# A batch's preparation spread over two steps of a software-pipelined attention and FFN kernel

## The chip, the cores and the metric

One core of one Trainium2 chip. The metric is the device time of one execution in microseconds (us), as the median of several runs. In what follows PE is TensorE, DVE is VectorE, ACT is ScalarE, POOL is GpSimd and SP is SyncE.

## The reference

The input x has 8 batches of 1024 tokens with 128 channels. Cut to what matters:

```python
def proj(W, b): return heads(x + x @ W.T + b)          # 16 heads of 8 channels
q, k1, k2, v1, v2 = proj(Wq, bq), proj(Wk1, bk1), ...
S1 = k1^T v1 / n; S2 = k2^T v2 / n                      # per head, over all 1024 tokens
y1 = q @ S1 * mean(v2); y3 = q @ S2 * mean(v1)
y2 = (S1 * S2).sum(rows); y4 = q @ (S1 * S2)
a = layernorm(y1 * g1 + y2 * g2 + y3 * g3 + y4 * g4) * ln_g + ln_b
x = layernorm(x + a @ Wo.T + bo)                        # "x1"
h = relu(x @ w1[0] + b1[0]); e = h @ w2[0] + b2[0]      # only expert 0 has weight
out = layernorm(layernorm(x + e) * gamma + beta)        # "y2", "y3", "res"
```

S1 and S2 are sums over all tokens of a batch. They are computed from the batch's Gram matrix x^T x (128x128) and its column sums. The attention of a batch then collapses to one 128x128 matrix P, applied to each token.

## The kernel before, in words

**Groups and steps.** A group is 512 tokens (four tiles of 128), so there are two groups to a batch and 16 in all. The program is a loop over steps n = -2 to 15, unrolled, written once for each engine. Each engine has its own instruction stream, runs it strictly in the written order, and the streams are tied by semaphores alone. In step n the engines work on several groups: `product(n+1)` (x of group n+1 times PQ, 16 matmuls into `z_ps`), `up(n, 0..3)` (the FFN's first layer of group n, three matmuls each), `turn_x(n+2)` (four transposes into `turn_ps`), the down projection of group n (16 fp32 products that the profile counts as 32), and `turn_x1(n+1)`. In the odd steps 1, 3 and 5 a Gram matrix (of batches 5 to 7) follows the down projection, in two halves around `turn_x1`.

**Preparation.** Batch b is prepared in the even step n = 2b - 2 (b = 2 to 7), in this chain:

- `split_G(b)` on POOL writes `G_hi` and `G_lo`, the Gram matrix in two parts, at the end of the even step before;
- `gram_av(b)` on PE (three matmuls into `prep_ps`, in the middle of `product`) waits for both parts;
- `e_and_v(b)` on DVE writes `E_sb`, in the middle of the normalization to `y2n`;
- `ak_e(b)` on PE (after `up(n, 0)`) waits for `E_sb`; `s_out(b)` on DVE writes `S_sb`;
- `prepare(b)` on POOL: gv, then S12, T, S12g, M_half and `M_sb`, all small elementwise instructions, at the head of POOL's step;
- `attention_matrix(b)` on PE (after half of the down projection) waits for `M_sb`; `PT_copy` on ACT; `centered(b)` on PE waits for that copy; `PQ_upper` on ACT and `PQ_rest` on DVE give PQ, which `product` of the next step needs.

**POOL's order in a step.** `prepare` (even steps), `result_bias(n-2)` (L532 `mr4`, L535 `nb4`; in odd steps it comes after y3), y2g (L567), y3 (L571), `xu` (L584), x1b2 (L595), x1beta (L597), and in even steps `split_G` (L549, L551). `result_bias(n-2)` waits for DVE's `rstd4` (L852).

**DVE's order around `rstd4`.** `xT_rest(n+2)` (L834, waits for ACT's `xT_hi`, which waits for `turn_x`), `rstd2` (L939), `rstd4` (L852), the normalization to `x1` (L821), `PQ_rest`, `add_y2(n)` (L865, waits for the down projection), statistics, x1T_lo (L963), then the next step's `rstd3`, `y2n`, y3 statistics, `s_out`, `rstd1` and so on.

**ACT's order.** std3, four squares, std1, four ReLUs (L708, `hT`), `xT_hi` (L699), std2 and std4, `PT_copy` (L677), `PQ_upper` (L683), the result (L690), `x1T_hi` (L757).

All matmuls stand on L1045 in the profile, since the helper `mm` issues them; the tile's name tells them apart.

Of the kernel before, what the change touches and what calls it, by code (L numbers as in the profile page):

```python
# [35 lines left out]
SEQ_TILES = SEQ // TILE  # L36
# [10 lines left out]
def build(nc, x, Wq, bq, Wk1, bk1, Wk2, bk2, Wv1, bv1, Wv2, bv2, g1, g2, g3, g4, ln_g, ln_b, Wo, bo,  # L47
# [11 lines left out]
    with ctx:  # L59
# [45 lines left out]
        warm = sb("warm", [128, 1])  # L105
        minus = sb("minus", [128, TILES])
# [85 lines left out]
        const_set = sem("const_set")  # L192
        consts = sem("consts")
# [64 lines left out]

        end_y2 = sem("end_y2")
# [144 lines left out]
        class Step:  # L404
            def __init__(self, n):

                self.n, self.s = n, n % 2

                def has(k):
                    return 0 <= n + k < GROUPS  # L410

                self.cur, self.prev, self.prev2 = has(0), has(-1), has(-2)
                self.last = n == GROUPS - 1
                self.nxt, self.nxt2 = has(1), has(2)

                self.prep = n == -1 or (n != 0 and n % 2 == 0 and has(2))
                self.ready = 1 if n == 0 else self.prepared() if self.prep and n != -1 else None
                self.gram = EARLY + n // 2 if n in (1, 3, 5) else None
                self.v_set = {0: 0, 7: 1}.get(n)
                self.v_rest = {0: 0, 7: 1}.get(n)  # L420

            def prepared(self):

                return self.n + 2 if self.n < 0 else self.seq(2)

# [16 lines left out]
        def _(sp):  # L442
# [25 lines left out]
            def store(b):  # L468
                for g in range(1 if b == BATCHES - 1 else SEQ_GROUPS):
                    if (b, g) in ((0, 0), (2, 1)):  # L470
                        place_v(b // 2)
                    wait(sp, res_out, b * SEQ_GROUPS + (g + 1))
                    sp.dma_start(out_v[b, :, g * TILES:(g + 1) * TILES, :], res[g][:, :, :]).then_inc(res_free[g], 16)
# [13 lines left out]
        def _(pool):  # L487
# [65 lines left out]
            def body(st):  # L553
# [10 lines left out]
                if st.prev:  # L564

                    wait(pool, y2n_out, n)
                    pool.tensor_tensor(y2g[:, :, :], y2n[:, :, :], rows(gamma_rows[:, :]), ALU.mult).then_inc(y2g_out, 1)  # L567
                    wait(pool, y2g_out, n)
                    wait(pool, x1beta_out, n)
                    wait(pool, res_out, n - 2)  # L570
                    pool.tensor_tensor(y3[(s - 1) % 2][:, :, :], y2g[:, :, :], x1beta[(s - 1) % 2][:, :, :], ALU.add).then_inc(y3_out, 1)  # L571
                if st.prev2 and not st.prep and not st.last:
                    result_bias(n - 2)
                if st.nxt2:

                    m = n + 2
                    b, g = st.seq(2), s
                    pool.wait_ge(x_loaded[b], 16)
                    if n == -1:
                        pool.wait_ge(x0_second, 16)  # L580
                    if st.n == -2:
                        pool.wait_ge(u_ready, 1)
                    wait(pool, y1_out, m - 1)
                    pool.tensor_tensor(xu[s % 2][:, :, :], X[:, b, g * TILES:(g + 1) * TILES, 0:C],  # L584
                                       rows(u_rows[:, :]), ALU.add).then_inc(xu_out, 1)
                if st.n == -1:
                    prepare(pool, 1)
# [11 lines left out]
                if st.cur and n % 2 == 0 and n // 2 + 2 < BATCHES:  # L599
                    split_G(n // 2 + 2)  # L600

# [3 lines left out]
            pool.wait_ge(y3_out, GROUPS - 1)  # L605
# [8 lines left out]
        def _(act):  # L614
# [94 lines left out]

            def body(st):  # L710
# [12 lines left out]
                if st.cur:  # L723
                    if st.n == 0:
                        act.wait_ge(ffn_rows, FFN_ROWS)
                    relu(st, 0)
                    relu(st, 1)
                    if st.last:
                        root3(n)
                    relu(st, 2)  # L730
                    relu(st, 3)
# [13 lines left out]
                if st.prep:  # L745
                    PT_copy(st.prepared())
# [25 lines left out]

            half_std(st3, std3, 0, end_st3, end_std3)
            act.wait_ge(end_nb, 1)
            act.wait_ge(y2g_out, GROUPS - 1)
# [3 lines left out]
            root4(GROUPS - 2)  # L779
# [8 lines left out]
        def _(dve):  # L788

            dve.wait_ge(consts, 2)  # L790
# [52 lines left out]
            def y3_stats(m, buf):  # L843
                wait(dve, y3_out, m + 1)
                wait(dve, mr4_out, m)
                stats(lambda i: pairs(y3[buf], i), st4, st4_out)
# [20 lines left out]

            def e_and_v(b):
# [16 lines left out]
            def body(st):  # L885
                n, s = st.n, st.s
                if st.prev:

                    wait(dve, std3_out, n)
                    dve.reciprocal(rstd3[:, :], std3[:, :]).then_inc(r3_out, 1)  # L890
                    wait(dve, r3_out, n)
                    wait(dve, y2g_out, n - 1)
                    normalize(y2n, y2_tile, st3, rstd3, y2n_out, (lambda: e_and_v(st.prepared())) if st.prep else None)
# [13 lines left out]
                if st.prep and st.n >= 0:  # L907
                    s_out(dve, st.prepared())
# [42 lines left out]
                if st.ready is not None and st.n >= 0:  # L951
                    PQ_rest(st.ready)
                if st.cur and st.nxt2:
                    add_y2(n, s)
# [70 lines left out]

            half_y2(0)
            half_r3(0)
            dve.scalar_tensor_tensor(out=nb_end[:, half[0]], in0=st3[:, 0, 1:6:3], scalar=-1.0,
                                     in1=rstd3[:, half[0]], op0=ALU.mult, op1=ALU.mult).then_inc(end_nb, 1)
            y3_stats(GROUPS - 2, 1 - own)  # L1030
            half_y2(1)
            y2d_second()
            result_factors(GROUPS - 2)
            result_bias_here(GROUPS - 2)
# [8 lines left out]
        def _(pe):  # L1043
# [3 lines left out]
            def keep_warm(times):  # L1047

                for _ in range(times):
                    mm(up_ps[1][:, 0:128], ident[:, :], ident[:, :])  # L1050
# [35 lines left out]
            def gram(b, tiles):  # L1086
# [8 lines left out]
                if b >= EARLY:  # L1095
                    pe.wait_ge(PQfix_out, b - EARLY + 2)
                for t in tiles:
# [19 lines left out]
            def gram_av(b):  # L1117

                if b >= 2:

                    wait(pe, G_out, min(BATCHES, b + 4))
                    if b == 5:
                        pe.wait_ge(rows_out, 2)
# [13 lines left out]
            def v_rows(v):  # L1137
# [3 lines left out]
                if v == 1:  # L1141
                    pe.wait_ge(PQfix_out, 5)
                mm(rows_bank(v)[0:VSET, 0:256], G_sb[:, b:b + VSET, C], A_kv[:, 1:3, :].rearrange("p j c -> p (j c)")).then_inc(rows_done, 1)

            def attention_matrix(b):

                wait(pe, M_out, (b + 1) * 2)
                pe.wait_ge(AqT_ready, 2)
                mm(prep_ps[:, 0:XW], M_sb[:, :], AqT[:, :], start=True, stop=False)
# [57 lines left out]
            def body(st):  # L1207
                n, s = st.n, st.s
                if st.n == -2:
                    pe.wait_ge(consts, 1)  # L1210
                    keep_warm(6)
# [21 lines left out]
                if st.n == -1:  # L1233
                    gram(2, range(2, 4))
                    product(0, 0)
                    turn_x(1)
                    gram(2, range(4, SEQ_TILES))
# [7 lines left out]
                if st.nxt:  # L1245
                    product(n + 1, st.seq(1), (lambda: gram_av(st.prepared())) if st.prep else None)
                if st.cur:
                    up(n, 0)
                if st.prep:
                    ak_e(st.prepared())  # L1250
                if st.v_set is not None:
                    v_rows(st.v_set)
                if st.cur:
                    up(n, 1)
                    up(n, 2)
                    up(n, 3)
                if st.nxt2:
                    turn_x(n + 2)
                if st.cur:
# [5 lines left out]
                    for t in range(TILES):  # L1265
# [3 lines left out]
                        if t == 2 and st.prep:  # L1269
                            attention_matrix(st.prepared())  # L1270
                        for k in range(FCH):
                            if t == 2 and k == 2 and st.prep:
                                centered(st.prepared())
                            if t == 0:
                                wait(pe, relu_out, n * FCH + (k + 1))
                            last = mm(to, hT[:, k, t * TILE:(t + 1) * TILE], w2_sb[:, k, :],
# [37 lines left out]
```

## Time and profile before

| | |
|---|---|
| median of 3 runs | 203.22 us (203.04 to 203.26) |
| the profiled execution | 202.93 us, of which the span from first to last instruction is 201.2 us |
| busy share of the span | PE 95%, DVE 78%, POOL 70%, ACT 64% |
| mean granted TensorE clock | 0.984 of full speed |

"Busy" is the time in which an engine has at least one instruction under way. The ends of matmuls are modelled and neighbours overlap, so a PE that waits a tenth of a microsecond still looks busy. Of one step that has room for nothing else, only the sum of its pieces tells whether PE waited.

### The profile page before, as it was taken

Reading aid. Unit: us, or ns where it says so; the run is one execution under the profiler, and the core shown is the slowest. Engines: PE = TensorE matmul, PEld = TensorE weight load, DVE = VectorE, ACT = ScalarE, POOL = GpSimd, SP = SyncE. Lnnn points to the kernel's source line nnn. Section 1 sums busy time; section 2 is a strip of 40 time slices with the busy share of each in tenths; the row PEclk is TensorE's granted clock in tenths of the full one; section 3 lists DMA queues with packets and bytes.
Section 4 is the critical chain, followed back from the end, with each engine's and each line's share of the span. In section 5 each row is a group of like instructions: output and inputs, shape, how many; then the busy total and the mean of one; then the engine's idle time right before and its main releaser. Section 6 shows DMA issues by size and latency. Waiting matters only on the chain.

```text
span 201.2 us, 4296 instructions
## 1 busy us (share of the span) xinstructions
PE 190.6 (95%) x1369; PEld 174.4 (87%) x1369; DVE 156.9 (78%) x470; ACT 129.1 (64%) x386; POOL 141.6 (70%) x191
## 2 busy tenths in 40 slices
PE   6999999999999999999999999999999999999930
PEld 6898979999898989999997989898989899988820
DVE  0286717988879796988879896989698969897683
ACT  0433456553859565975768685867597759786852
POOL 8627490675599838984698859985998598876450
PEclk9999999999999999999999999999999999999985
DMA  5999502000001100101010300110010101010012
GB/s 169 199 285 286 134 0 82 3 2 3 0 3 49 55 2 0 57 0 52 3 52 28 104 3 0 54 53 4 0 52 5 52 3 52 2 52 30 25 54 104
DMA packets 12641, 10.64 MB, mean 53 GB/s; under 512 B 730, under 2 KB 10475, under 8 KB 12619
## 3 DMA queue, kind: packets, MB, share of 16 engines
q1 hardware_dynamic: 11960, 9.32, 15.0%
q0 software_dynamic: 352, 0.92, 2.2%
q8 instruction: 11, 0.18, 0.4%
q10 hardware_dynamic: 306, 0.13, 0.2%
q14 instruction: 12, 0.09, 0.2%
HBM read 6.17 MB, written 4.20 MB: 52 GB/s over the span
## 4 chain that ended last, share of the span: by engine, by line
PE 86%; DVE 6%; issue 3%; POOL 2%; ACT 1%; DVEq 0%; POOLq 0%
PE down_ps L1045 25%; PE up_ps L1045 25%; PE z_ps L1045 14%; PE prep_ps L1045 13%; PE turn_ps L1204 3%; PE turn_ps L1175 3%; DVE st L814 1%; DVE down_ps L865 1%; POOL y2g L567 1%; POOL y L571 1%; DVE z_ps L925 1%; ACT res L690 1%; DVE y2n L821 1%; PE z_ps L1055 0%; DVE res L1022 0%
## 5 line engine op out<-in xcount | busy, mean ns | idle before, releaser
L1045 PE MATMUL down_ps<-w_sb,hT 128*128 128x128 f32 x480 | 58.9, 276 | 0.1
L1045 PEld LDWEIGHTS down_ps<-w_sb,hT 128*128 128x128 f32 x480 | 56.4, 192 | 0.7 <-ACT hT L708 0.3
L708 ACT ACTIVATE hT<-up_ps,cols 128x512 f32<-128x512 f32 x64 | 42.2, 682 | 5.2 <-PE up_ps L1045 5.0
L690 ACT ACTIVATE res<-y,nb,rstd 128x128 f32<-128x128 f32 x60 | 24.8, 483 | 6.6 <-POOL nb L535 5.9
L595 POOL TENSOR_TENSOR x1b<-x,b_rows 128x512 f32<-128x512 f32 x16 | 20.6, 1286 | 10.4 <-DVE x L821 10.4
L1045 PE MATMUL up_ps<-x1T_hi,w_hi 128*128 128x512 f32 x64 | 26.1, 408 | 0.0
L1045 PE MATMUL up_ps<-x1T_lo,w_hi 128*128 128x512 f32 x64 | 25.4, 398 | 0.0
L1045 PE MATMUL up_ps<-x1T_hi,w_lo 128*128 128x512 f32 x64 | 25.3, 395 | 0.0
L567 POOL TENSOR_TENSOR y2g<-y2n,gamma_rows 128x512 f32<-128x512 f32 x15 | 19.2, 1282 | 4.8 <-DVE y2n L821 4.8
L821 DVE TENSOR_SCALAR x<-z_ps,st,rstd 128x128 f32<-128x128 f32 x64 | 21.9, 404 | 0.1
L657 ACT ACTIVATE z_sq<-z_ps 128x128 f32<-128x128 f32 x64 | 16.8, 270 | 7.7 <-PE z_ps L1045 7.7
L821 DVE TENSOR_SCALAR y2n<-down_ps,st,rstd 128x128 f32<-128x128 f32 x60 | 21.0, 403 | 0.5
L584 POOL TENSOR_TENSOR xu<-X,u_rows 128x512 f32<-128x512 f32 x16 | 19.0, 1189 | 2.4 <-DVE u_rows L810 2.4
L597 POOL TENSOR_TENSOR x1beta<-x,beta_rows 128x512 f32<-128x512 f32 x16 | 20.6, 1289 | 0.0
L571 POOL TENSOR_TENSOR y<-y2g,x1beta 128x512 f32<-128x512 f32 x15 | 19.1, 1272 | 1.2
L1045 PE MATMUL z_ps<-PQ_hi,xT_hi 128*128 128x256 f32 x64 | 19.3, 302 | 0.0
L925 DVE SCALAR_TENSOR_TENSOR z_ps<-z_ps,rstd,xu 128x128 f32<-128x128 f32 x64 | 18.1, 352 | 0.6
L1045 PE MATMUL z_ps<-PQ_hi,spread 128*128 128x256 f32 x64 | 18.0, 281 | 0.1
L1045 PE MATMUL z_ps<-PQ_hi,xT_lo 128*128 128x256 f32 x64 | 18.1, 282 | 0.0
L1045 PE MATMUL z_ps<-PQ_lo,xT_hi 128*128 128x256 f32 x64 | 18.0, 282 | 0.0
L649 ACT ACTIVATE std<-st,eps_col 128x4 f32<-128x4 f32 x46 | 12.4, 295 | 7.0 <-DVE st L814 7.0
L757 ACT ACTIVATE x1T_hi<-turn_ps 128x512 fp32r<-128x512 f32 x16 | 9.4, 589 | 11.2 <-PE turn_ps L1175 10.9
(170 smaller groups left out, 417.0 us busy)
## 6 DMA issues: line engine op xcount, KB each, us to landing
out<-res SPq DMA_DIRECT2D x15, 256.0 KB, 2.0
X<-in_L_attn_x SPq DMA_DIRECT2D x7, 512.0 KB, 8.7
V_all<-V_dram SPq DMA_DIRECT2D x6, 128.0 KB, 3.0
X<-in_L_attn_x SPq DMA_DIRECT2D x2, 256.0 KB, 3.5
w_sb<-in_L_ffn_w POOLq DMA_DIRECT2D x2, 256.0 KB, 7.8
out<-res SPq DMA_DIRECT2D x2, 128.0 KB, 2.2
w_raw<-in_L_attn_Wv ACTq DMA_DIRECT2D x2, 64.0 KB, 2.3
w_raw<-in_L_attn_Wk SPq DMA_DIRECT2D x2, 64.0 KB, 3.2
```

Of the source, the lines that this page charges most:

```text
L567: pool.tensor_tensor(y2g[:, :, :], y2n[:, :, :], rows(gamma_rows[:, :]), ALU.mult).then_inc(y2g_out, 1)
L571: pool.tensor_tensor(y3[(s - 1) % 2][:, :, :], y2g[:, :, :], x1beta[(s - 1) % 2][:, :, :], ALU.add).then_inc(y3_out, 1)
L584: pool.tensor_tensor(xu[s % 2][:, :, :], X[:, b, g * TILES:(g + 1) * TILES, 0:C], rows(u_rows[:, :]), ALU.add).then_inc(xu_out, 1)
L595: pool.tensor_tensor(x1b2[(s + 1) % 2][:, :, :], x1[:, :, :], rows(b2_rows[:, :]), ALU.add).then_inc(x1b2_out, 1)
L597: pool.tensor_tensor(x1beta[(s + 1) % 2][:, :, :], x1[:, :, :], rows(beta_rows[:, :]), ALU.add).then_inc(x1beta_out, 1)
L649: act.activation(dst[:, :], src, ACT.Sqrt, bias=eps_col[:, :], scale=scale).then_inc(done, 1)
L657: act.activation(z_sq[:, t, :], z_ps[t // 2][:, t % 2 * 256:t % 2 * 256 + C], ACT.Square, accum_out=z_sum[:, t:t + 1]).then_inc(sq_out, 1)
L690: last = act.activation(res[buf][:, t, :], y3[buf][:, t, :], ACT.Identity, scale=rstd4[:, t:t + 1], bias=nb4[:, t:t + 1])
L708: act.activation(hT[:, k, :], up_ps[k % len(up_ps)][:, :], ACT.Relu, bias=cols[:, 5 + k:6 + k]).then_inc(relu_out, 1)
L821: last = dve.tensor_scalar(dst[:, t, :], of_tile(t), st[:, t // 2, 3 * (t % 2) + 1:3 * (t % 2) + 2], rstd[:, t:t + 1], ALU.subtract, ALU.mult)
L925: last = dve.scalar_tensor_tensor(out=y1_tile(t), in0=y1_tile(t), scalar=rstd1[:, t:t + 1], in1=xu[(s + 1) % 2][:, t, :], op0=ALU.mult, op ...
L1045: return pe.matmul(o, lhsT, rhs, start=start, stop=stop)
```

## The change

The three parts of the preparation that make E and S move to the odd step before (n = 2b - 3, `st.pre` and `early()`): `gram_av` in its `product`, `ak_e` after its `up(n, 3)`, `e_and_v` in its `y2n`, `s_out` before its `add_y2`. `prepare` stays at the head of POOL's even step. `attention_matrix` moves up to stand between `up(n, 3)` and `turn_x`, `PT_copy` between the ReLUs and `xT_hi`, and `centered` before the second quarter of the down projection. `split_G` moves ahead of x1b2 and x1beta in POOL's even step. The second set of V rows, and its trip through DRAM on SP's queue, move from step 7 to step 6. At the start, seven warming matmuls on a tile that DVE sets take the place of six on `ident`, and `product(0)` comes two Gram tiles later. At the end, DVE makes y3 of group 14 (`y2d_before`, `y3_before`) where POOL did, the last ReLU is cut into two halves, and DVE takes the statistics of that y3 before the half sums of group 15.

The diff, cut to its core:

```diff
         self.ready = 1 if n == 0 else self.prepared() if self.prep and n != -1 else None
+        self.pre = n % 2 == 1 and n > 0 and self.seq(3) < BATCHES
         self.gram = EARLY + n // 2 if n in (1, 3, 5) else None
-        self.v_set = {0: 0, 7: 1}.get(n)
-        self.v_rest = {0: 0, 7: 1}.get(n)
+        self.v_set = {0: 0, 6: 1}.get(n)
+        self.v_rest = {0: 0, 6: 1}.get(n)
...
         return self.n + 2 if self.n < 0 else self.seq(2)
+    def early(self):
+        return self.seq(3)
...
         for g in range(1 if b == BATCHES - 1 else SEQ_GROUPS):
-            if (b, g) in ((0, 0), (2, 1)):
+            if (b, g) in ((0, 0), (2, 0)):
                 place_v(b // 2)
...
             result_bias(n - 2)
-        if st.prev:
+        if st.prev and not st.last:
...
                                rows(u_rows[:, :]), ALU.add).then_inc(xu_out, 1)
+        if st.cur and n % 2 == 0 and n // 2 + 2 < BATCHES:
+            split_G(n // 2 + 2)
         if st.n == -1:
...
-        if st.cur and n % 2 == 0 and n // 2 + 2 < BATCHES:
-            split_G(n // 2 + 2)
     run_steps(body)
...
     pool.wait_ge(end_y2n, 1)
-    pool.wait_ge(y3_out, GROUPS - 1)
+    pool.wait_ge(y3_out, GROUPS - 2)
     pool.tensor_tensor(y2g[:, 0:2, :], y2n[:, 0:2, :], rows(gamma_rows[:, :], 2), ALU.mult).then_inc(end_y2g, 1)
...
         act.activation(hT[:, k, :], up_ps[k % len(up_ps)][:, :], ACT.Relu, bias=cols[:, 5 + k:6 + k]).then_inc(relu_out, 1)
+    def relu_half(st, k, h):
+        part = slice(h * GROUP // 2, (h + 1) * GROUP // 2)
+        wait(act, up_done, st.n * FCH + (k + 1))
+        act.activation(hT[:, k, part], up_ps[k % len(up_ps)][:, part], ACT.Relu,
+                       bias=cols[:, 5 + k:6 + k]).then_inc(relu_out, 1)
...
             relu(st, 2)
-            relu(st, 3)
+            if st.last:
+                for h in range(2):
+                    relu_half(st, 3, h)
+            else:
+                relu(st, 3)
+        if st.prep and st.n >= 0:
+            PT_copy(st.prepared())
         if st.nxt2 and st.n >= 0:
...
             root4(n - 2)
-        if st.prep:
+        if st.prep and st.n < 0:
             PT_copy(st.prepared())
...
+    root4(GROUPS - 2)
     half_std(st3, std3, 0, end_st3, end_std3)
     act.wait_ge(end_nb, 1)
-    act.wait_ge(y2g_out, GROUPS - 1)
+    act.wait_ge(y2g_out, GROUPS - 2)
     for t in range(2):
...
     last.then_inc(end_y2n, 1)
-    root4(GROUPS - 2)
     half_std(st3, std3, 1, end_st3, end_std3)
...
+    dve.memset(warm_in[:, :], 1.0).then_inc(warm_set, 1)
     dve.wait_ge(consts, 2)
...
     def y3_stats(m, buf):
-        wait(dve, y3_out, m + 1)
+        if m == GROUPS - 2:
+            dve.wait_ge(y3_last, 1)
+        else:
+            wait(dve, y3_out, m + 1)
         wait(dve, mr4_out, m)
...
                           x1b2[s % 2][:, :, :], ALU.add).then_inc(y2_out, 1)
+    def y2d_before(m):
+        wait(dve, sq_out, GROUPS * TILES)
+        wait(dve, std1_out, GROUPS)
+        wait(dve, st3_out, m + 1)
+        for t in range(TILES):
+            last = dve.scalar_tensor_tensor(out=y2d[:, t, :], in0=y2_tile(t),
+                                            scalar=st3[:, t // 2, 3 * (t % 2) + 1:3 * (t % 2) + 2],
+                                            in1=gamma_rows[:, :], op0=ALU.subtract, op1=ALU.mult)
+        last.then_inc(y2d_out, 1)
+    def y3_before(m, buf):
+        dve.wait_ge(y2d_out, 1)
+        wait(dve, x1beta_out, m + 1)
+        wait(dve, res_out, m - 1)
+        for t in range(TILES):
+            last = dve.scalar_tensor_tensor(out=y3[buf][:, t, :], in0=y2d[:, t, :],
+                                            scalar=rstd3[:, t:t + 1], in1=x1beta[buf][:, t, :],
+                                            op0=ALU.mult, op1=ALU.add)
+        last.then_inc(y3_last, 1)
...
         n, s = st.n, st.s
+        if st.last:
+            y2d_before(n - 1)
         if st.prev:
...
             wait(dve, r3_out, n)
+        if st.last:
+            y3_before(n - 1, (s - 1) % 2)
+        if st.prev and not st.last:
             wait(dve, y2g_out, n - 1)
-            normalize(y2n, y2_tile, st3, rstd3, y2n_out, (lambda: e_and_v(st.prepared())) if st.prep else None)
+            normalize(y2n, y2_tile, st3, rstd3, y2n_out, (lambda: e_and_v(st.early())) if st.pre else None)
         if st.prep and st.n == -2:
...
             split_w1()
-        if st.prep and st.n >= 0:
-            s_out(dve, st.prepared())
         if st.n == -2:
...
             PQ_rest(st.ready)
+        if st.pre:
+            s_out(dve, st.early())
         if st.cur and st.nxt2:
...
+    y3_stats(GROUPS - 2, 1 - own)
     half_y2(0)
+    result_factors(GROUPS - 2)
+    result_bias_here(GROUPS - 2)
     half_r3(0)
...
                              in1=rstd3[:, half[0]], op0=ALU.mult, op1=ALU.mult).then_inc(end_nb, 1)
-    y3_stats(GROUPS - 2, 1 - own)
     half_y2(1)
     y2d_second()
-    result_factors(GROUPS - 2)
-    result_bias_here(GROUPS - 2)
     y3_second()
...
         for _ in range(times):
-            mm(up_ps[1][:, 0:128], ident[:, :], ident[:, :])
+            mm(up_ps[1][:, 0:128], warm_in[:, :], warm_in[:, :])
...
             pe.wait_ge(PQfix_out, b - EARLY + 2)
+            pe.wait_ge(S_out, b - EARLY + 3)
         for t in tiles:
...
-            wait(pe, G_out, min(BATCHES, b + 4))
-            if b == 5:
-                pe.wait_ge(rows_out, 2)
+            wait(pe, G_out, min(BATCHES, b + 3))
             if b == 2:
...
         if v == 1:
-            pe.wait_ge(PQfix_out, 5)
+            pe.wait_ge(S_out, 5)
         mm(rows_bank(v)[0:VSET, 0:256], G_sb[:, b:b + VSET, C], A_kv[:, 1:3, :].rearrange("p j c -> p (j c)")).then_inc(rows_done, 1)
...
         pe.wait_ge(AqT_ready, 2)
+        if b >= 2:
+            wait(pe, G_out, min(BATCHES, b + 4))
+        if b == 4:
+            pe.wait_ge(rows_out, 2)
         mm(prep_ps[:, 0:XW], M_sb[:, :], AqT[:, :], start=True, stop=False)
...
         if st.n == -2:
+            pe.wait_ge(warm_set, 1)
+            keep_warm(7)
             pe.wait_ge(consts, 1)
-            keep_warm(6)
             pe.wait_ge(consts, 2)
...
         if st.n == -1:
-            gram(2, range(2, 4))
+            gram(2, range(2, 6))
             product(0, 0)
             turn_x(1)
-            gram(2, range(4, SEQ_TILES))
+            gram(2, range(6, SEQ_TILES))
             gram(3, range(SEQ_TILES))
...
         if st.nxt:
-            product(n + 1, st.seq(1), (lambda: gram_av(st.prepared())) if st.prep else None)
+            product(n + 1, st.seq(1), (lambda: gram_av(st.early())) if st.pre else None)
         if st.cur:
             up(n, 0)
-        if st.prep:
-            ak_e(st.prepared())
         if st.v_set is not None:
...
             up(n, 3)
+        if st.pre:
+            ak_e(st.early())
+        if st.prep:
+            attention_matrix(st.prepared())
         if st.nxt2:
...
                     turn_x1(n + 1, False)
-                if t == 2 and st.prep:
-                    attention_matrix(st.prepared())
                 for k in range(FCH):
-                    if t == 2 and k == 2 and st.prep:
+                    if t == 1 and k == 0 and st.prep:
                         centered(st.prepared())
...
                         wait(pe, relu_out, n * FCH + (k + 1))
+                    if st.last and t == 2 and k == 0:
+                        pe.wait_ge(relu_out, GROUPS * FCH + 1)
                     last = mm(to, hT[:, k, t * TILE:(t + 1) * TILE], w2_sb[:, k, :],
```

## Rows read from the trace of the kernel before

**Rows 1.** The page's chain by engine, and all of PE's waits (total, times, longest).

```profile
PE 86%; DVE 6%; issue 3%; POOL 2%; ACT 1%; DVEq 0%; POOLq 0%
...
PE up_ps L1045 <- POOL ident L492: 1.6, 1, 1.6
```

**Rows 2.** Chain that ended last, steps 9 and 10: start, us, what (from end to end).

```profile
125.20 1.89 PE z_ps L1045 x16
...
129.90 0.44 PE turn_ps L1204 x4
130.34 3.57 PE down_ps L1045 x32
...
134.35 0.94 PE z_ps L1045 x8
135.29 0.36 PE prep_ps L1045 x3
...
137.33 0.71 PE prep_ps L1045 x4
...
142.37 0.49 PE prep_ps L1045 x4
...
143.42 0.95 PE prep_ps L1045 x4
...
146.14 0.24 PE z_ps L1045 x2
```

**Rows 3.** The same chain, in step 1: half a Gram matrix.

```profile
45.48 0.90 PE prep_ps L1045 x8
```

**Rows 4.** Timeline of POOL, steps 9 and 10: start us, us, what, and idle before.

```profile
128.03 0.28 POOL L549 CAST G_hi<-G_sb 128x128 fp32r<-128x128 f32 x1
128.39 0.46 POOL L551 TENSOR_TENSOR G_lo<-G_sb,G_hi 128x128 fp32r<-128x128 f32 x1
...
132.13 0.20 POOL L532 TENSOR_TENSOR mr<-st,rstd 128x4 f32<-128x4 f32 x1 [0.68 <-DVE rstd L852]
...
136.21 0.74 POOL L376 TENSOR_TENSOR gv<-V_all,gmask 128x256 f32<-128x256 f32 x1
139.18 0.46 POOL L380 TENSOR_TENSOR S<-S_sb 128x128 f32<-128x128 f32 x1 [2.23 <-DVE S_sb L361]
...
141.75 0.46 POOL L396 TENSOR_TENSOR M_sb<-M_half,S12g 128x128 f32<-128x128 f32 x1
142.31 0.20 POOL L532 TENSOR_TENSOR mr<-st,rstd 128x4 f32<-128x4 f32 x1
...
145.32 1.20 POOL L584 TENSOR_TENSOR xu<-X,u_rows 128x512 f32<-128x512 f32 x1
```

**Rows 5.** Timeline of all engines in step 10, from `turn_x` to `rstd4`.

```profile
139.99 0.60 PE L1204 MATMUL turn_ps<-ident,X 128*128 128x128 f32 x4
...
140.77 0.59 ACT L699 ACTIVATE xT_hi<-turn_ps 128x512 fp32r<-128x512 f32 x1
...
142.09 0.15 DVE L852 RECIPROCAL rstd<-std 128x4 f32<-128x4 f32 x1
```

**Rows 6.** The same chain, at the start: the first half of Gram matrix 0.

```profile
4.51 1.73 PE prep_ps L1045 x8
```

**Rows 7.** PE's weight loads in step -1: the one for `turn_x1(0)`.

```profile
25.37 0.42 PEld L1175 LDWEIGHTS turn_ps<-ident,x 128*128 128x128 f32 x4 [0.37 <-DVE x L821]
```

**Rows 8.** Timeline of DVE, the last step and what follows it.

```profile
187.41 0.16 DVE L852 RECIPROCAL rstd<-std 128x4 f32<-128x4 f32 x1
...
190.94 0.43 DVE L982 TENSOR_TENSOR prep_ps<-prep_ps,x1b 128x256 f32<-128x256 f32 x1 [1.08 <-PE prep_ps L1045]
...
192.59 0.76 DVE L814 BATCH_NORM_STATS2 st<-y 128x6 f32<-128x256 f32 x2
...
194.26 0.61 DVE L996 SCALAR_TENSOR_TENSOR z_sq<-z_ps,st,gamma_rows 128x128 f32<-128x128 f32 x2
...
195.91 0.76 DVE L1014 BATCH_NORM_STATS2 st<-y 128x6 f32<-128x256 f32 x2
```

More of the change, by code:

```diff
@@ L105, in build @@
         warm = sb("warm", [128, 1])
+        warm_in = sb("warm_in", [128, 128])
         minus = sb("minus", [128, TILES])
@@ L192, in build @@
         const_set = sem("const_set")
+        warm_set = sem("warm_set")
         consts = sem("consts")
@@ L257, in build @@
         res_out = sem("res_out")
+        y2d_out = sem("y2d_out")
+        y3_last = sem("y3_last")
         end_y2 = sem("end_y2")
```

## The prediction

> **What bounds the kernel now.** I read the chain that ended last and the table of waits first. The chain is 86% PE, and PE's only listed wait is the one for `ident` at the start [rows 1]. From the first step to the last, the time is therefore the sum of what PE is given plus small waits hidden in its pieces. So I read the chain for two steps without a Gram matrix, 9 and 10 [rows 2]. An odd step takes 134.35 - 125.20 = 9.15 us: product, up, `turn_x`, down, `turn_x1`. Both steps take 146.14 - 125.20 = 20.94. Twice 9.15 is 18.30; the other 2.64 is the preparation: `gram_av` 0.36, `ak_e` 0.71, attention 0.49, `centered` 0.95 and some 0.13 of switching. The 0.71 for four passes is long: four transposes of the same width take 0.44. Some 0.2 to 0.3 is a wait for `E_sb`.
>
> Next I read POOL's timeline [rows 4], because POOL sits between the two halves of the preparation. It idles 2.23 before S12, until `S_sb` is there, then ends `M_sb` at 142.21 and goes straight on to `mr4` at 142.31. The question for the change is where this idle time goes. Last, the way from `turn_x` to `rstd4` over ACT and DVE [rows 5], because `mr4` waits for `rstd4` and all of POOL's step stands behind `mr4`.
>
> **The preparation on PE.** Apart from a warming matmul, nothing is added to PE's work; blocks move. `ak_e` behind `up(n, 3)` no longer waits (`E_sb` is two microseconds old) and no longer splits the up products. I take 0.40 for it, 0.40 for attention (up to 0.49 now, with a short wait), 0.95 and 0.36 for the others: 2.11 in place of 2.64, so 0.5 less in each of the three pairs without a Gram matrix (steps 7 to 12). In the three pairs with one, PE comes later to `ak_e` and mostly the split is saved: 0.15 each. Together **-1.9** (bounds -1.2 and -2.4).
>
> **First new wait: attention for `M_sb`.** In the new order the chain from `turn_x` of the odd step is:
>
> - `turn_x` to `mr4`: now 142.31 - 139.99 = 2.32 [rows 4, 5]. ACT starts `xT_hi` 0.78 after `turn_x` because the fourth ReLU runs first. With `ak_e` or attention ahead of `turn_x`, that ReLU is done up to 0.4 sooner in relation to it. So the bounds are 1.9 and 2.3; I take 2.15, since the transposes need most of that time themselves.
> - `mr4` to the head of `prepare` (nb4, xu, x1b2, x1beta): 136.21 - 132.13 = 4.08 [rows 4].
> - `prepare` without its wait: 0.74 for gv, and from S12 to the end of `M_sb` 142.21 - 139.18 = 3.03: 3.77. It is not moved, and its length does not change. What goes is the wait for S alone.
> - 0.07 to hand over, as from `rstd4` to `mr4` [rows 4, 5].
>
> Together 10.07. PE gets from `turn_x` to the new place of attention in one bare step, 9.15: down, `turn_x1`, product, up. So PE waits **0.92** in steps 8, 10 and 12. In steps 2, 4 and 6 the Gram matrix of the step before gives PE two times 0.90 more [rows 3], 10.95 in all, and nothing is left to wait for. Behind attention stand `turn_x`, down and everything else of PE; they all slip.
>
> **Second new wait: `gram_av` for `G_lo`.** `split_G` used to have a step in hand; now `gram_av` follows in the next product. From `turn_x` of the even step: 2.15 to `mr4`; `mr4` to the end of `xu` 146.52 - 142.31 = 4.21; `split_G` 128.85 - 128.03 = 0.82; hand-over 0.07: 7.25. POOL's 2.2 of idle time is not won: it moves from before S12 to before `mr4`. PE's way is 135.29 - 129.90 = 5.39 plus `centered` 0.95 = 6.34 [rows 2]. PE waits **0.91** in steps 3, 5, 7, 9 and 11 (batches 3 to 7; batch 2 is split in step 0, long before). Behind it stand half the product, up and `turn_x`, so the first chain starts later by as much and does not get shorter.
>
> Sum of the waits: 3 x 0.92 + 5 x 0.91 = **+7.3**. Over eight waits the bounds 1.9 and 2.3 give 5.3 to 8.5.
>
> **Cover of the rest.** DVE gives up 1.0 in even steps and has it in odd ones; `s_out` fits in its wait for the down projection, and PE reaches `turn_x` later there, so it still waits for `xT_hi`. If that cover failed, `rstd4` would slip by up to 0.4. `PT_copy` has `turn_x` and a quarter of down (0.44 + 0.9) before `centered`, against 0.9 needed. The V rows and SP's three loads come a step before `gram_av(5)` and two before their use; SP stores nothing earlier for it. The Gram matrices' new wait for `S_out` ends as down ends (0 to 0.2, three times; I take 0).
>
> **The ends.** At the start PE can begin about 0.5 sooner, but the seventh warming matmul fills most of it. The first Gram half runs at 1.73 for eight passes, against 0.90 later [rows 3, 6]; if PE comes to the fast pace sooner, up to 0.5 is won. The two Gram tiles ahead of `product(0)` fill PE's wait for PQ, but `turn_x1(0)` already waits 0.37 for DVE [rows 7] and would only wait longer: 0. I take **-0.3** (0 to -0.6). At the end DVE's way from its first half sum to the statistics of y3 is 195.91 - 190.94 = 4.97 [rows 8]. The y3 statistics (0.7) leave it, and `rstd4` with its bias fills the wait for std3. DVE needs eight instructions of 0.3 (0.61 for two) more beforehand. From 187.6 that is 2.4 + 0.2 + 0.7, which ends at about 190.9, just in time. **-0.8** (-0.3 to -1.0). PE's gain from the half ReLU, about 0.3, is hidden behind DVE.
>
> **Sum.** The profiled execution took 202.93; + 7.3 - 1.9 - 0.3 - 0.8 = 207.2, span 205.5. The median shown is 0.29 above it, so **207.4** for the median, with a range of its own of 205.0 to 209.2.
>
> **Rivals.**
>
> - *It does what it says* (faster). No wait comes in the place of the old ones, and the 3.0 of savings stay: 200.2. For it: PE is the bound, and POOL idles 2.2 per pair. It needs POOL's results 0.9 sooner than the rows give, for instance `turn_x` to `mr4` in 1.25 rather than 2.15. Against it: POOL's chain is one instruction after another. 14%.
> - *Only `gram_av` waits*, because `prepare` profits from something that I do not see: 203.2 + 4.55 - 3.0 = 204.8. 14%.
> - *Only attention waits*, because `split_G` is sooner: 203.2 + 2.8 - 3.0 = 203.0, between a little faster and the same. 5%.
> - *The waits bring the clock down.* The mean granted clock is 0.984 with hardly a wait on PE, and eight waits of 0.9 are new. Gram passes at the slow and the fast pace differ by 1.73 to 0.90; if 1 us of work after each wait ran slow, it would cost 0.9 x 8 = 7 more: 214. 5%. The Trainium skill, "TensorE: Matmul & The Clock Gate", section "A second HAM failure mode: psum-queue depth-cycling", describes frequent short pauses of PE that make its clock swing between the two levels. By that rule this rival would be the likely one; in this trace PE has hardly a pause that could show it.
>
> My forecast has the other 62%. Faster by over 0.2% (0.4 us, about what a measurement of this kernel can tell): 14 + 3 = 17%. The same: 3%. Slower: 80%. The range from 202.6 to 209.2 leaves out the first and the last rival, 19%.
>
> **What would show it.** In the new profile, PE's waits should name POOL's `M_sb` three times and `G_lo` five times, each about 0.9; steps 9 and 10 together should take 22.2 in place of 20.94; POOL's wait before S12 should be gone and one of about 2.6 before `mr4` in even steps be there; steps 1 and 2 should be no longer than before; and the time from the last matmul to the end should shrink by 0.5 to 0.8. The prediction is wrong if PE passes from `up(n, 3)` to attention without a gap in step 10, or if a pair takes about 20.4.

## The result, and the profile after

The changed kernel takes 208.74 us in the median of four executions (208.57 to 209.70), the kernel before 203.13 beside it (202.59 to 203.26): a ratio of 1.0289, 95% interval 1.0250 to 1.0328. The profiled execution took 208.89, with a span of 207.2 where it was 201.2. Executions over 1.5% above the fastest of the same kernel are left out of all times and ratios here (242.57 and 242.21 us of the kernel before, 233.89 us of the kernel in experiment 4).

First the page of the kernel after: busy time, the granted clock in 40 slices, and the chain by engine.

```profile
PE 190.6 (92%) x1371; PEld 174.6 (84%) x1371; DVE 158.7 (77%) x475; ACT 130.9 (63%) x387; POOL 138.9 (67%) x189
...
PEclk9999999999999999999999999999999999999996
...
PE 52%; POOL 19%; DVE 9%; issue 8%; ACT 7%; DMA 2%; SPq 1%; DVEq 0%; POOLq 0%; ACTq 0%
```

PE's share of the chain fell from 86% [rows 1] to 52%, and POOL's rose from 2% to 19%, though POOL is busy for 67% of the span only, less than before. An engine with a third of its time free sets the pace, since its instructions lie one behind another between two of PE's. All of PE's waits (total, times, longest) say where:

```profile
PE prep_ps L1094 <- POOL G_lo L560: 4.3, 5, 0.9
PE prep_ps L1094 <- POOL M_sb L400: 2.2, 3, 0.7
PE up_ps L1094 <- DVE warm_in L810: 1.1, 1, 1.1
PE turn_ps L1227 <- DVE x L842: 0.4, 1, 0.4
PE z_ps L1104 <- DMA w_raw<-in_L_attn_Wk: 0.2, 1, 0.2
```

Now PE's timeline from `turn_x` of step 7 to `turn_x` of step 9, and the end of step 10. These answer to [rows 2] and [rows 5].

```profile
112.78 0.60 PE L1256 MATMUL turn_ps<-ident,X 128*128 128x128 f32 x4
...
122.83 0.49 PE L1094 MATMUL prep_ps<-AqT,M_sb 128*128 128x130 f32 x2 [0.74 <-POOL M_sb L400]
...
123.30 0.63 PE L1256 MATMUL turn_ps<-ident,X 128*128 128x128 f32 x4
...
124.66 1.03 PE L1094 MATMUL prep_ps<-center,PT_sb 128*128 128x256 f32 x4
...
128.20 0.60 PE L1227 MATMUL turn_ps<-ident,x 128*128 128x128 f32 x4
...
130.63 0.36 PE L1094 MATMUL prep_ps<-A_hi,G_hi 128*128 128x256 f32 x1 [0.88 <-POOL G_lo L560]
...
134.81 0.60 PE L1094 MATMUL prep_ps<-E_sb,A_kv 128*128 128x128 f32 x4
135.25 0.60 PE L1256 MATMUL turn_ps<-ident,X 128*128 128x128 f32 x4
...
150.67 0.60 PE L1227 MATMUL turn_ps<-ident,x 128*128 128x128 f32 x4
```

From `turn_x1` at the end of step 8 (128.20) to that of step 10 (150.67) it is 22.47 us; before it was 20.93. PE stands still behind the up projection until `M_sb` is there, and in the middle of `product` until `G_lo` is. `turn_x` follows `ak_e` and attention in 0.44 to 0.47, so no other wait hides in those places.

The same stretch in POOL's timeline, from `mr4` of step 7 on; it answers to [rows 4].

```profile
114.97 0.20 POOL L541 TENSOR_TENSOR mr<-st,rstd 128x4 f32<-128x4 f32 x1 [1.84 <-DVE rstd L876]
...
119.04 0.73 POOL L380 TENSOR_TENSOR gv<-V_all,gmask 128x256 f32<-128x256 f32 x1
119.74 0.46 POOL L384 TENSOR_TENSOR S<-S_sb 128x128 f32<-128x128 f32 x1
...
122.32 0.45 POOL L400 TENSOR_TENSOR M_sb<-M_half,S12g 128x128 f32<-128x128 f32 x1
125.52 0.20 POOL L541 TENSOR_TENSOR mr<-st,rstd 128x4 f32<-128x4 f32 x1 [2.74 <-DVE rstd L876]
...
128.52 1.19 POOL L593 TENSOR_TENSOR xu<-X,u_rows 128x512 f32<-128x512 f32 x1
129.66 0.29 POOL L558 CAST G_hi<-G_sb 128x128 fp32r<-128x128 f32 x1
130.03 0.46 POOL L560 TENSOR_TENSOR G_lo<-G_sb,G_hi 128x128 fp32r<-128x128 f32 x1
```

The wait of 2.23 before S12 [rows 4] is gone and one of 2.74 stands before `mr4`. POOL finishes `M_sb`, PE goes on to `turn_x`, POOL has nothing to do until `rstd4` comes back 2.7 us later, and then PE waits for POOL.

### The profile page after: what moved, and what is told of

Read it like the earlier page. It is cut to its first block, busy times and chain, and to the rows that moved or that the text cites. A ratio compares the mean times of both kernels' runs of the same rounds, so it can differ in the third digit from the quotient of the medians.

```text
span 207.2 us, 4306 instructions
## 1 busy us (share of the span) xinstructions
PE 190.6 (92%) x1371; PEld 174.6 (84%) x1371; DVE 158.7 (77%) x475; ACT 130.9 (63%) x387; POOL 138.9 (67%) x189
## 4 chain that ended last, share of the span: by engine, by line
PE 52%; POOL 19%; DVE 9%; issue 8%; ACT 7%; DMA 2%; SPq 1%; DVEq 0%; POOLq 0%; ACTq 0%
PE up_ps L1094 16%; PE down_ps L1094 11%; PE prep_ps L1094 10%; PE z_ps L1094 10%; POOL xu L593 4%; POOL y2g L576 3%; PE turn_ps L1256 3%; ACT hT L716 2%; ACT xT_hi L707 2%; POOL x1b L606 2%; DMA w_raw<-in_L_attn_Wk 2%; POOL x1beta L608 2%; PE turn_ps L1227 2%; DVE xT_lo L855 1%; DVE x L842 1%
## 5 line engine op out<-in xcount | busy, mean ns | idle before, releaser
L1094 PE MATMUL down_ps<-w_sb,hT 128*128 128x128 f32 x480 | 57.4, 275 | 0.1
L716 ACT ACTIVATE hT<-up_ps,cols 128x512 f32<-128x512 f32 x63 | 41.6, 681 | 2.5 <-PE up_ps L1094 2.3
L1094 PE MATMUL up_ps<-x1T_hi,w_hi 128*128 128x512 f32 x64 | 25.6, 400 | 0.0
L541 POOL TENSOR_TENSOR mr<-st,rstd 128x4 f32<-128x4 f32 x14 | 2.8, 199 | 32.1 <-DVE rstd L876 32.1
L855 DVE TENSOR_TENSOR xT_lo<-turn_ps,xT_hi 128x512 fp32r<-128x512 f32 x16 | 11.0, 690 | 14.5 <-ACT xT_hi L707 14.5
L576 POOL TENSOR_TENSOR y2g<-y2n,gamma_rows 128x512 f32<-128x512 f32 x14 | 18.0, 1286 | 3.7 <-DVE y2n L842 3.7
L842 DVE TENSOR_SCALAR y2n<-down_ps,st,rstd 128x128 f32<-128x128 f32 x56 | 19.7, 404 | 0.5
L580 POOL TENSOR_TENSOR y<-y2g,x1beta 128x512 f32<-128x512 f32 x14 | 17.9, 1277 | 1.1
```

Of the source, the lines that this page charges most:

```text
L716: act.activation(hT[:, k, :], up_ps[k % len(up_ps)][:, :], ACT.Relu, bias=cols[:, 5 + k:6 + k]).then_inc(relu_out, 1)
L842: last = dve.tensor_scalar(dst[:, t, :], of_tile(t), st[:, t // 2, 3 * (t % 2) + 1:3 * (t % 2) + 2], rstd[:, t:t + 1], ALU.subtract, ALU.mult)
L855: dve.tensor_tensor(xT_lo[:, :], turn_ps[:, :], xT_hi[:, :].bitcast(f32), ALU.subtract).then_inc(xTlo_out, 1)
L1094: return pe.matmul(o, lhsT, rhs, start=start, stop=stop)
```

## Experiments

In each difference, "-" and "+" are against the changed kernel unless said otherwise, and "..." marks a cut. The kernels named together ran beside the same executions of the kernel before; those had a median of 202.85 for the first four, 203.13 for the next four and 202.76 for the last, so the ratios compare. One thing must be taken out of the traces: `turn_x1(0)`, the end of the start, begins at 24.55 to 25.73 in the profiled executions of kernels whose start is the same. Small effects are therefore read from there to `turn_x1` of the last group; that stretch takes 165.48 in the changed kernel (25.17 to 190.65).

### 1. `split_early`: POOL splits the Gram matrix before `mr4`

```diff
                     prepare(pool, st.prepared())
+                    if n // 2 + 2 < BATCHES:
+                        split_G(n // 2 + 2)
                     if st.prev2:
                         result_bias(n - 2)
...
-                if st.cur and n % 2 == 0 and n // 2 + 2 < BATCHES:
-                    split_G(n // 2 + 2)
+                if st.n == 0:
+                    split_G(2)
```

> The changed kernel (208.7 us, pairs of steps of 22.47), with split_G placed right behind prepare in POOL's even step, where POOL idles 2.74 us before mr4. Theory (POOL's chain from turn_x over mr4, y2g, y3, xu and split_G to gram_av sets the odd step's wait): G_lo is ready 7 us earlier, the five waits of 1.1 us before gram_av go, the three before attention stay: 203.1 (202.5 to 203.9). Rival A (DVE's E and S in the odd step delay rstd4, and POOL only shows it): DVE's work is the same, so no more than 1 us is won: 207.7 to 208.7. Rival B (the new order of PE's blocks is dearer in itself): 208.7.

Measured: 203.45 us (203.16 to 204.26), ratio 1.0037 (1.0019 to 1.0056). PE's first wait in the list:

```profile
PE prep_ps L1096 <- POOL M_sb L400: 2.3, 3, 0.8
```

`G_lo` has left the list, and the split now falls into the 2.7 us in which POOL was idle. Some 0.8 us of work moved past `mr4`, y2g, y3 and `xu` are worth 5.1 us (1.0289 less 1.0037), 1.0 for each of the five waits. In the trace the stretch from `turn_x1(0)` on is 5.4 shorter (160.07), 1.1 for each. That is most of what the change had cost.

### 2. `xu_first`: `xu` before `mr4` in odd steps

```diff
-                if st.prev2 and not st.prep and not st.last:
-                    result_bias(n - 2)
                 if st.nxt2:
...
                                        rows(u_rows[:, :]), ALU.add).then_inc(xu_out, 1)
+                if st.prev2 and not st.prep and not st.last:
+                    result_bias(n - 2)
```

> The changed kernel with xu ahead of mr4 and nb4 in POOL's odd steps, where POOL idles 1.84 us before mr4. Theory (the chain from turn_x over mr4, nb4, xu, x1b2, x1beta and prepare to M_sb sets the wait before attention): the chain is 1.15 shorter, the wait of 0.9 in steps 8, 10 and 12 goes, the five before gram_av stay: 208.7 - 3 x 1.0 = 205.7 (205.2 to 206.3). Rival A (DVE) and B (PE's order): 208.7.

Measured: 207.67 us (207.48 to 208.46), ratio 1.0256 (1.0219 to 1.0293). The medians differ by 1.1, the ratios by 0.3%, 0.7 us, and the intervals of the two ratios overlap. That is less than a quarter of the 3.0 expected, and outside the range given. `xu` takes 1.2, but attention's wait shrinks only from 0.74 to 0.50. POOL in step 9 of this kernel shows what came in between:

```profile
134.83 1.18 POOL L591 TENSOR_TENSOR xu<-X,u_rows 128x512 f32<-128x512 f32 x1
136.71 0.20 POOL L541 TENSOR_TENSOR mr<-st,rstd 128x4 f32<-128x4 f32 x1 [0.69 <-DVE rstd L876]
136.98 0.20 POOL L544 TENSOR_TENSOR nb<-mr,minus 128x4 f32<-128x4 f32 x1
138.04 1.27 POOL L606 TENSOR_TENSOR x1b<-x,b_rows 128x512 f32<-128x512 f32 x1 [0.86 <-DVE x L842]
```

With `xu` out of the way, x1b2 is ready before DVE has written x1, and waits 0.86 for it. DVE takes up x1 (1.37 for its four tiles) only after `rstd4`. From `mr4` to x1b2 it is now 138.04 - 136.71 = 1.33, and was 116.54 - 114.97 = 1.57: of the 1.2 taken off POOL's way, 0.24 is won, and then the way over DVE is the longer one. Three times 0.24 is 0.7. The trace shows just that: the stretch from `turn_x1(0)` on takes 164.73, 0.75 less. The rest of the 1.1 lies before it, since `turn_x1(0)` begins at 24.68 there and at 25.17 in the changed kernel. My expectation had not followed that second way.

### 3. `both_pool_edits`: the two together

> Both edits, split_G behind prepare and xu ahead of mr4 in odd steps. Theory: no wait is left, PE's blocks alone set a pair of steps (20.4), and what the change saves comes out: 208.7 - 5.6 - 3.0 = 200.1 (199.5 to 201), faster than the kernel before. Rival C (with POOL out of the way, DVE or ACT in the odd step is late next, by about 0.5 a pair): 202 to 203. Rival B: 208.7.

Measured: 202.65 us (202.12 to 203.12), ratio 0.9991 (0.9977 to 1.0005). The edits add up (2.5% and 0.3%), but the time is above the range expected and in that of rival C (202 to 203): again a wait is left over. Attention in step 10, in PE's timeline:

```profile
139.81 0.49 PE L1096 MATMUL prep_ps<-AqT,M_sb 128*128 128x130 f32 x2 [0.50 <-POOL M_sb L400]
```

POOL's x1b2 waits 0.86 for x1 here too, as in experiment 2, so the longer way to attention is now the one over DVE's x1; experiment 5 tests this.

### 4. `split_late`: the split where it was before the change

```diff
-                if st.cur and n % 2 == 0 and n // 2 + 2 < BATCHES:
-                    split_G(n // 2 + 2)
...
                     pool.tensor_tensor(x1beta[(s + 1) % 2][:, :, :], x1[:, :, :], rows(beta_rows[:, :]), ALU.add).then_inc(x1beta_out, 1)
+                if st.cur and n % 2 == 0 and n // 2 + 2 < BATCHES:
+                    split_G(n // 2 + 2)
```

> The changed kernel with split_G back at the end of POOL's even step, behind x1b2 and x1beta, 2.5 us later. Theory: each of the five waits before gram_av grows by 2.5: 208.7 + 12.5 = 221 (219.5 to 222), the waits before attention stay. Rivals A and B: 208.7, since gram_av has other work before it.

Measured: 229.02 us in one execution, so this has no interval. It is above the range expected (219.5 to 222). First PE's waits for `G_lo`. Then PE's timeline at one of them. Then two windows after it (length, busy time of PE, its weight loads, DVE, ACT and POOL, granted clock, DMA share and GB/s):

```profile
PE prep_ps L1095 <- POOL G_lo L560: 18.1, 6, 3.3
```

```profile
120.52 0.55 PE L1095 MATMUL prep_ps<-A_hi,G_hi 128*128 128x256 f32 x1 [3.29 <-POOL G_lo L560]
...
121.30 0.41 PE L1095 MATMUL z_ps<-PQ_hi,xT_hi 128*128 128x256 f32 x1
121.51 0.41 PE L1095 MATMUL z_ps<-PQ_hi,xT_lo 128*128 128x256 f32 x1
```

```profile
121.00:124.50 3.50, 3.50 (x17) 3.23 (x16) 2.04 (x7) 1.21 (x6) 1.68 (x2) 0.62 0.00 0
124.50:127.00 2.50, 2.50 (x17) 2.18 (x15) 1.84 (x6) 2.46 (x4) 0.89 (x1) 1.00 0.00 0
```

The wait grows by 2.4, as x1b2 and x1beta (1.28 each) are now ahead of the split, and batch 2's split comes too late as well. That gives 13.8 of the 20.3 us added. After the pause shown, matmuls of `product` start every 0.21 us instead of 0.12, and the clock granted over the next 3.5 us was 0.62 of full speed. This is the loss that my last rival had in mind, but at a wait three times as long. The other pauses divide it. After the four of 3.3 in steps 3, 5, 7 and 9 the granted clock over the next 3.5 us was 0.58 to 0.62, and each of these pairs of steps grew by 3.9 to 4.0, so by about 1.5 more than its wait. After the one in step 11, as long as the others, it was 1.00: matmuls start every 0.12 us again, and steps 11 and 12 grew by 2.4, the wait alone.

```profile
173.23 0.36 PE L1095 MATMUL prep_ps<-A_hi,G_hi 128*128 128x256 f32 x1 [3.28 <-POOL G_lo L560]
173.42 0.28 PE L1095 MATMUL prep_ps<-A_lo,G_hi 128*128 128x256 f32 x1
173.54 0.28 PE L1095 MATMUL prep_ps<-A_hi,G_lo 128*128 128x256 f32 x1
```

### 5. `prep_odd_step`: `prepare` in the odd step too

Against experiment 3: behind `mr4` and `nb4` of the odd step comes the preparation of M, so that it stands ahead of x1b2 and fills POOL's wait for x1.

```diff
-                    prepare(pool, st.prepared())
                     if n // 2 + 2 < BATCHES:
                         split_G(n // 2 + 2)
...
                 if st.prev2 and not st.prep and not st.last:
                     result_bias(n - 2)
...
+                if st.pre:
+                    prepare(pool, st.early())
```

> The kernel with both POOL edits, and prepare(b) moved out of the head of POOL's even step into the odd step before, behind mr4 and nb4 and ahead of x1b2. Theory (in the kernel with both edits POOL's x1b2 waits 0.86 for DVE's x1, and prepare stands behind it; that is what left three waits of 0.5 before attention): prepare then needs only S_sb, M_sb is ready 2 us before its place, the three waits go with the 0.1 of resuming each: 1.8 less than both edits, 200.8 where the kernel before takes 202.85. Rival C (DVE or ACT is late next, whatever POOL does): 202 to 202.6. Rival D (x1b2 and x1beta, now 3.7 later, hold up the next down sum or x1): 203 or more.

Measured: 200.19 us (199.89 to 201.06), ratio 0.9872 (0.9849 to 0.9895). POOL in step 7:

```profile
111.84 0.20 POOL L544 TENSOR_TENSOR nb<-mr,minus 128x4 f32<-128x4 f32 x1
112.00 0.73 POOL L380 TENSOR_TENSOR gv<-V_all,gmask 128x256 f32<-128x256 f32 x1
113.41 0.46 POOL L384 TENSOR_TENSOR S<-S_sb 128x128 f32<-128x128 f32 x1 [0.69 <-DVE S_sb L365]
...
116.01 0.46 POOL L400 TENSOR_TENSOR M_sb<-M_half,S12g 128x128 f32<-128x128 f32 x1
```

In PE's timeline, `turn_x1` at the ends of steps 8 and 10:

```profile
123.78 0.60 PE L1230 MATMUL turn_ps<-ident,x 128*128 128x128 f32 x4
...
144.12 0.60 PE L1230 MATMUL turn_ps<-ident,x 128*128 128x128 f32 x4
```

No wait for `M_sb` or `G_lo` is left on PE, and steps 9 and 10 take 144.12 - 123.78 = 20.34 together: what the prediction named as the sign of a pair without new waits (about 20.4). The preparation's blocks on PE therefore save 0.59 per pair; `ak_e` gives 0.27 of it (0.71 in [rows 2], 0.44 here) and attention 0.15 (0.49 and 0.34). The time is also that of the rival "it does what it says" (200.2), once the queue gives POOL's results in time.

### 6. `s_out_sooner`: the same, and `S_sb` earlier on DVE

Against experiment 5:

```diff
+                if st.pre:
+                    s_out(dve, st.early())
                 if st.nxt2 and st.n >= -1:
                     xT_rest(n + 2)
...
-                if st.pre:
-                    s_out(dve, st.early())
```

> The kernel with prepare in the odd step, and s_out ahead of xT_rest on DVE, where DVE idles 0.3 for xT_hi. Theory: the first half of each Gram matrix in steps 1, 3 and 5 took 1.06 in place of 0.90, since it waits for S_out; with S_sb 2.5 earlier these 0.16 go: 0.5 less in all, 200.3. Rival: xT_lo and x1 come 0.3 later and turn_x1 waits for x1: 0 to 1 us more than the kernel with prepare in the odd step.

Measured: 199.63 us (199.13 to 200.18), ratio 0.9831 (0.9806 to 0.9856), the shortest time of the study, 1.7% below the kernel before. The median is 0.56 below that of experiment 5, but the single times of the two overlap, so the traces must show what the edit did. The first half of a Gram matrix waits for `S_out`. In the chain it takes 1.06 in the changed kernel and 0.90 here, like the second half, which waits for nothing. First after, then this kernel:

```profile
46.07 1.06 PE prep_ps L1094 x8
47.57 0.90 PE prep_ps L1094 x8
```

```profile
46.36 0.90 PE prep_ps L1097 x8
```

The wait that I had put at nothing costs 0.16, three times. From `turn_x1(0)` to `turn_x1` of the last group, experiment 5's kernel takes 156.96 and this one 156.45: 0.51 less, three times 0.17.

### 7. `ends_alone`: the steps of before with the ends of after

> The kernel before with the ends of the changed one (warming on warm_in, two more Gram tiles ahead of product(0), y3 of group 14 on DVE, the halved ReLU, the statistics first) and its own steps 0 to 14. Theory: what the traces of before and after show at the ends is the whole effect there, 0.2 at the start and 0.65 from the last matmul on: 0.85 less, a ratio of 0.996; the steps alone then cost 6.5. Rival (the ends hurt too, or bring all of what was foreseen, 1.1 or more): a ratio of 1.000 or above, or under 0.994.

Measured: 202.16 us (201.47 to 202.49), ratio 0.9951 (0.9934 to 0.9969). Start and tail bring 1.0 us (0.6 to 1.3), beside 1.1 predicted.

### 8. `E_made_twice`: DVE writes E a second time, into a tile that nobody reads

> The changed kernel with DVE's instruction for E issued twice for batches 2 to 7, the first time into a tile that nobody reads: DVE has 0.4 more in each odd step 1 to 11. Theory: DVE idles 1.18 in these steps until xT_hi is there, so nothing comes later: 208.7 (208.3 to 209.1). Rival A (DVE's work moved into the odd step sets the end of the chain): 6 x 0.4 = 2.4 more, 211.

Measured: 208.93 us (208.54 to 209.38), ratio 1.0294 (1.0268 to 1.0319), against 1.0289 for the changed kernel. One more instruction in DVE's odd steps costs nothing that can be measured; from `turn_x1(0)` on the trace takes 165.48 with it and without. So it is not the load of E that DVE took over in odd steps which made them longer. The other instructions that it took over, those for `S_sb`, stand behind `rstd4` in DVE's order, and so cannot hold up `mr4`.

### 9. `before_xu_first`: experiment 2's edit in the kernel before

> The kernel before with xu ahead of mr4 and nb4 in POOL's odd steps, the edit that took 1.1 us from the changed kernel. Theory: in the kernel before, prepare waits 2.23 for S_sb, so a chain that is 1.1 shorter ahead of it is lost in that wait, and PE has nothing to wait for there: 203.1, a ratio of 1.000 within 0.002. Rival (POOL's order is worth something in itself, for instance because xu then collides less with DVE): faster by 0.3% or more, as in the changed kernel.

Measured: 203.10 us (202.32 to 203.78), ratio 1.0017 (0.9999 to 1.0035): nothing, or 0.3 more. Where the preparation has a step in hand, the order of `xu` and `mr4` doesn't matter; it matters only once PE waits for what is behind them.

## Why the prediction was right, and where its sizes were off

The forecast was 207.4 us, with a range of its own of 205.0 to 209.2, and 202.6 to 209.2 with the middle rivals; 208.74 was measured. (The sum gives 207.2 + 0.29 = 207.5; it was written down 0.1 too low.) The mechanism is the predicted one, shown from both sides: with the waits taken away by a new order the time falls below that of before (experiment 5), with one made longer it rises (experiment 4), and DVE's new load for E is excluded as the cause (experiment 8). Point by point, on the span, where 4.3 us were forecast and 6.0 came:

- **Attention waits for `M_sb`, three times 0.92.** It does, in steps 8, 10 and 12. From `turn_x` (112.78) to attention (122.83) it is 10.05, forecast 10.07; PE could have been there after 9.15, at 121.93. The wait is 0.90, and the two matmuls then take 0.49 where they take 0.38 without one. That 0.11 was not in my sum: 1.01 each. It could have been: in the kernel before, attention shows 0.49 in step 10 [rows 2] and 0.34 in step 2, but I took 0.40 for the new place and only the idle time for the wait. The idle time that the profile puts down (0.74) is less than either, as PE's ends are modelled.
- **`gram_av` waits for `G_lo`, five times 0.91.** It does, for batches 3 to 7 and not for batch 2. From `turn_x` (123.30) to it is 7.33, forecast 7.25: `mr4` came after 2.22 in place of 2.15, and the hand-over from the end of `G_lo` (130.49) to PE took 0.14 in place of 0.07. PE's way took 0.06 less, 6.28. That makes 1.05, and 0.07 to start again: 1.12 each. Both waits together are 8.6, where the sum had 7.3. This is the term that was most off.
- **Blocks on PE, -0.5 and -0.15 a pair.** -0.59 in pairs without a Gram matrix (experiment 5). In steps 3 and 4 the kernel of experiment 6 takes 22.13 and the kernel before the change 22.26: -0.13. Together these are 2.2 saved, where the sum had 1.9.
- **The Gram halves' wait for `S_out`, taken as 0 (0 to 0.2).** It is 0.16, near the upper bound (experiment 6): +0.5 in all. `s_out` does fit into DVE's wait for the down projection, but ends only 0.25 before that wait does: in step 3 at 69.24, and PE begins the Gram matrix 0.14 later, at 69.38, the same hand-over as from `G_lo`.
- **Steps 1 and 2 no longer than before.** +0.02, that is -0.15 and +0.16.
- **The second set of V rows** moves 0.7 us from step 7 to step 6 and changes no sum. It must be taken out before those pairs are compared.
- **The start, -0.3.** -0.2: `turn_x1(0)` begins at 25.17 and not 25.37 [rows 7], and it still waits for DVE. The chain at the start now hangs on the load of Wk, which lands at 6.3, so warming earlier has less to win.
- **The tail, -0.8.** -0.65, from `turn_x1` of the last group to the end (17.2 before, 16.55 now). Experiment 7 gives 1.0 for both ends together. I had PE's part hidden behind DVE; in the trace after, DVE waits for PE's last matmuls:

```profile
199.16 0.43 DVE L1031 TENSOR_TENSOR z_ps<-z_ps,x1b 128x256 f32<-128x256 f32 x1 [0.16 <-PE z_ps L1094]
```

- **The clock.** The rival needed a slow clock behind waits of 0.9. The page shows the granted clock at its upper tenth in 39 of 40 slices, mean 0.992, where it had been 0.984 (0.987 to 0.993 over the executions of after). The Trainium skill, "TensorE: Matmul & The Clock Gate", section "A second HAM failure mode: psum-queue depth-cycling", has short frequent pauses swing the clock; eight pauses of about 1 us, 8 to 24 us apart, did not do it here.

Term by term: 8 waits +8.6, Gram halves +0.5, blocks -1.8 and -0.4, start -0.2, tail -0.65, together +6.05 against 6.0 measured. The pairs of steps show the same when they are read alone: 1.12 for steps 3 and 4, 1.54 and 1.53 for 9 to 12, beside -0.15 + 0.16 + 1.12 = 1.13 and -0.59 + 1.01 + 1.12 = 1.54.

Not settled: what the 0.07 and 0.11 after a wait are. They are read from the starts of neighbouring matmuls, and no run here changes only them. The 0.49 does not go with the length of the wait: it is the same after 0.74 and after 0.50 (experiment 3). Experiment 4's loss to the clock is one execution, and why the pause in step 11 cost nothing there stays open.

## What to carry to other kernels

- A producer that has slack in its share of busy time can still be late. When work is moved ahead on the engine that consumes it, follow the chain from the last thing the consumer itself gave (here `turn_x`) over every engine to the new place, and compare it with the consumer's own way there. This gave the wait to within 0.02 and 0.14 us.
- If such a wait appears, look for what stands ahead of the short, urgent instruction in its engine's queue and can wait. 0.8 us of POOL's work, moved to where POOL idled, was worth 5 us. The change as it stood was slower by 2.9%; with POOL's queue put in the order of the new deadlines it was faster than the kernel before by 1.3%, and by 1.7% with `S_sb` earlier on DVE.
- The gain of the second such edit is not the length of what was moved (1.2), but the distance to the next chain (0.24).

## What the runs showed of the hardware

- In experiment 4, four of five PE pauses of 3.3 us were followed by 3.5 us at a granted clock of 0.58 to 0.62, a mix of the two levels, 1.2 and 2.4 GHz; the fifth (step 11) and the one of 1.5 us in step 1 were followed by 1.00. Pauses of about 1 us left it at 1.00; this is from `up` of step 8 to `turn_x` of step 9 in the changed kernel, columns as above:

```profile
119.00:136.00 17.00, 15.38 (x105) 13.67 (x104) 13.81 (x43) 12.12 (x37) 13.30 (x18) 1.00 0.04 17
```

- At the end two DVE instructions take 0.96 us for what took 0.61 before, and POOL's y3 runs at the same time. DVE first, then POOL:

```profile
200.89 0.96 DVE L1056 SCALAR_TENSOR_TENSOR y<-z_sq,rstd,x1beta 128x128 f32<-128x128 f32 x2
```

```profile
200.71 0.72 POOL L618 TENSOR_TENSOR y<-y2g,x1beta 128x256 f32<-128x256 f32 x1
```

  In experiments 1, 6 and 7 these ran together too, and it took 0.96 each time. In the kernel before the two did not meet (DVE, then POOL), and DVE took 0.61:

```profile
195.26 0.61 DVE L1007 SCALAR_TENSOR_TENSOR y<-z_sq,rstd,x1beta 128x128 f32<-128x128 f32 x2
```

```profile
194.29 0.72 POOL L610 TENSOR_TENSOR y<-y2g,x1beta 128x256 f32<-128x256 f32 x1
```

  This adds 0.35 to DVE's way in the tail. The Trainium skill, "GPSIMD Engine Reference", section "1. Specifications", says that GpSimd shares its SBUF interfaces with VectorE and contends with DVE instructions that have two SBUF inputs; both inputs of these are in SBUF, and the rows agree.
